# Making the w1 and w2 products of a finished tile inside the Mamba pass of the next one

## The chip, the cores and the metric

One core of a Trainium2 chip runs the whole program. The metric is device time in microseconds (us): before the change the median of three runs was 3416.43 us (3415.66 to 3416.49). TensorE is called PE here, VectorE DVE, ScalarE ACT, GpSimd POOL and SyncE SP.

## The reference

A Mamba block, then a feed-forward network (FFN) with ternary weights; each adds its input and is followed by a layer norm without weights. Input x is (4, 2048, 256) in float32.

```python
xz = x @ in_proj_w.T; xc, z = xz[..., :512], xz[..., 512:]
u = silu(causal_conv4(xc) + conv_b)
dt_lo, B, C = split(u @ x_proj_w.T)                 # 64, 16, 16
delta = softplus(dt_lo @ dt_proj_w.T + dt_proj_b)
h_t = exp(delta_t * A) * h_{t-1} + delta_t * u_t * B_t
y = (sum_n h * C + u * D) * silu(z)
x1 = layernorm(x + y @ out_proj_w.T)
g = silu((x1 @ w1.T) * s1) * ((x1 @ w2.T) * s2)     # 256 -> 1024
g = gelu((g @ h1.T) * sh1); g = gelu((g @ h2.T) * sh2)   # 1024 -> 1024
out = layernorm(x1 + (g @ w3.T) * s3)               # 1024 -> 256
```

## The kernel before

The work is cut into 16 tiles of 512 positions (4 sequences of 4 tiles). Three parts follow each other, with a barrier between.

**Mamba stage** (`mamba_stage`). A tile holds 64 groups of 128 lanes (32 channels x 4 states). For each group ACT makes the decays exp(delta*A) in one of three PSUM banks (`decay_of`, L560), and DVE runs the scan over 512 positions (L753). For every four groups DVE (L738) or POOL (L640) makes delta*u*B, POOL multiplies the states by C (L630), PE sums over the states (`fold_step`, L409). The order on each engine is written out as 64 slots per pass, numbered i = 0 to 63; a pass also makes the front of the next tile: the convolution (slots 0 to 15), silu of u on ACT (17) and of z (40), the products for z (26 to 33), for x of the tile after the next (47 to 53), the step sizes (24, 38, 54, 6) with their softplus in pieces over seven slots, and the output projection (55 to 60) with the residual sums (58, 59, 61, 62). The layer norm of a tile stands at slots 1 to 11 of the next pass. Each engine works through its slots in order and waits on counting semaphores. SP's queue carries the copies that spread delta and delta*u over partitions through DRAM (`copies`, L245 to L262), the load of x (L284) and the store of x1 (L295). ACT issues no DMA.

**Rounding of the weights** (`round_weights`). All five FFN weights are loaded in 28 pieces, rounded to fp32r on ACT, compared with the unrounded ones on DVE, and the differences are summed on PE. A flag says whether all survived exactly. If so, the split stage below runs, else a float32 stage. With these inputs it is the split stage.

**FFN stage** (`ffn_stage` with `split`). An activation is kept as two fp32r parts, the rounded one ("high", made by a copy on ACT, L1053) and the rest ("low", a subtraction on DVE, L1117), and each product runs over both parts. For each tile PE transposes x1 (L967), makes 8 chunks of w1 and w2 products (64 matmuls, L955), layer 0 (128 matmuls), layer 1 (128) and the output product (L1014). ACT applies silu (L1060) and gelu (L1076), DVE the gate (L1127), the residual and the norm. Two PSUM banks alternate in each layer: product m waits until gelu m-2 has emptied its bank. The w1 and w2 products of the next tile come after the output product of this one.

## Time and profile before

| | |
|---|---|
| median of 3 runs | 3416.43 us |
| the profiled execution, its time / its span | 3414.18 us / 3412.4 us |
| Mamba stage | 0 to about 2034 us |
| rounding of the weights | about 2034 to 2072 us |
| FFN stage | about 2072 to 3412 us |
| busy over the span | PE 78%, DVE 69%, ACT 53%, POOL 50% |
| granted TensorE clock, mean | 0.86 |

The profile is one execution. Busy time leaves out register, branch and DMA-issuing instructions. Row 2 of the profile's page shows two regimes: in slices 1 to 23 DVE and POOL are at 8 to 9 tenths, PE at 5 to 7 and the granted clock at 7 to 8 tenths; from slice 26 on PE is at 9 and the clock at 9 to 10. In timeline rows the bracket at the end gives the idle time before an instruction and who ended it. A float32 matmul is recorded twice.

### The profile page before, as it was taken

To read this page: it belongs to the slowest core of one execution; us is meant where nothing else is said; L and a number is where in the kernel's file an instruction comes from. 1 tells how busy PE (TensorE), PEld (TensorE's weight loads), DVE (VectorE), ACT (ScalarE), POOL (GpSimd) and SP (SyncE) were. 2 spreads that over 40 slices of the span, in tenths; PEclk is the share of its full clock that TensorE was granted. 3 is DMA by queue.
4 is the path that set the end of the run, shared out by engine and by line. 5 is a ranking of instruction groups with operands and counts; after the bars stand their busy time and mean duration, and the time that the engine had idled before them with its cause. 6 is when DMAs were issued, how large, how long until landed. Compare 5 with 4: busy or idle time off the path is not lost. (4 is left out here: it accounts for less than half of the span.)

```text
span 3412.4 us, 36441 instructions
## 1 busy us (share of the span) xinstructions
PE 2663.4 (78%) x10431; PEld 1545.8 (45%) x10432; DVE 2371.1 (69%) x2860; ACT 1819.3 (53%) x2980; POOL 1702.9 (50%) x636
## 2 busy tenths in 40 slices
PE   5766776676676667657667438999999999999997
PEld 2222222122122122212212115888888888888886
DVE  2999999899999899999999964333334334344443
ACT  3657666666666666666666534444444444444442
POOL 0888888898898888888888850000000000000000
PEclk8777877788787787778878657999999999999999
DMA  3344433444433444334444322000000000000000
GB/s 89 80 99 111 111 94 88 104 105 99 107 93 91 105 111 100 91 94 105 99 111 98 88 85 97 13 13 12 13 12 13 12 13 12 13 12 13 12 13 13
DMA packets 138266, 225.74 MB, mean 66 GB/s; under 512 B 14432, under 2 KB 49120, under 8 KB 138080
## 3 DMA queue, kind: packets, MB, share of 16 engines
q1 hardware_dynamic: 138080, 223.80, 26.4%
q14 instruction: 135, 1.11, 0.1%
q8 instruction: 51, 0.84, 0.1%
HBM read 173.42 MB, written 50.33 MB: 66 GB/s over the span
## 5 line engine op out<-in xcount | busy, mean ns | idle before, releaser
L753 DVE TENSOR_TENSOR_SCAN h<-bank,state,db 128x512 f32<-128x512 f32 x1024 | 1255.9, 1273 | 84.6 <-POOL hc L630 61.0
L630 POOL TENSOR_TENSOR hc<-h,c_rows 128x2048 f32<-128x2048 f32 x256 | 1159.2, 4533 | 85.1 <-DVE h L753 48.8
L560 ACT ACTIVATE bank<-d_bc,a_neg 128x512 f32<-128x512 f32 x1024 | 699.1, 687 | 595.0 <-DVE h L753 594.0
L955 PE MATMUL s_bank<-s_act,weights_r 128*128 128x512 f32 x4096 | 935.0, 389 | 0.0
L955 PEld LDWEIGHTS s_bank<-s_act,weights_r 128*128 128x128 f32 x4096 | 767.8, 188 | 158.6
L1117 DVE TENSOR_TENSOR s_act<-s_h,s_act 128x512 fp32r<-128x512 f32 x384 | 262.8, 689 | 638.0 <-ACT s_act L1053 625.1
L388 PE MATMUL bank<-bc,w_spread 64*128 64x512 f32 x272 | 157.3, 602 | 449.4 <-DVE db L738 445.7
L1076 ACT ACTIVATE s_h<-s_bank,s_sc 128x512 f32<-128x512 f32 x256 | 176.0, 687 | 528.8 <-PE s_bank L955 528.6
L738 DVE TENSOR_TENSOR db<-bank,du_bc 128x2048 f32<-128x2048 f32 x192 | 436.5, 2273 | 19.8 <-DMA du_bc<-du_rows 19.8
L409 PE MATMUL bank<-hc,fold_w 128*32 128x512 f32 x2048 | 358.9, 782 | 93.5 <-DVE uz L777 78.0
L388 PEld LDWEIGHTS bank<-bc,w_spread 64*128 64x128 f32 x272 | 59.4, 232 | 658.1 <-DVE db L738 571.3
L640 POOL TENSOR_TENSOR db<-du_bc,b_row 128x2048 f32<-128x2048 f32 x64 | 289.5, 4524 | 127.2 <-DVE h L753 90.8
L347 PE MATMUL bank<-xb,w_conv 128*128 128x512 f32 x512 | 291.3, 699 | 6.3 <-DVE res L784 4.6
L1053 ACT ACTIVATE s_act<-s_h 128x512 fp32r<-128x512 f32 x384 | 241.7, 629 | 18.1 <-DVE s_h L1127 9.9
L955 PE MATMUL s_bank<-s_x_t,weights_r 128*128 128x512 f32 x1024 | 236.8, 391 | 1.4 <-DVE s_x_t L1111 1.4
L955 PEld LDWEIGHTS s_bank<-s_x_t,weights_r 128*128 128x128 f32 x1024 | 192.3, 189 | 41.2 <-DVE s_x_t L1111 1.8
L1060 ACT ACTIVATE s_silu<-s_bank,s_sc 128x512 f32<-128x512 f32 x128 | 88.3, 690 | 178.8 <-PE s_bank L955 170.9
L409 PEld LDWEIGHTS bank<-hc,fold_w 128*32 128x32 f32 x2048 | 44.7, 120 | 304.1 <-issue 188.4
L347 PEld LDWEIGHTS bank<-xb,w_conv 128*128 128x128 f32 x512 | 99.7, 215 | 172.8 <-issue 164.8
L322 PE MATMUL bank<-xT_sb,w_in 128*128 128x512 f32 x256 | 147.8, 719 | 19.8 <-DVE a_neg L724 15.7
L361 PE MATMUL bank<-uz,w_xp 128*96 128x512 f32 x128 | 87.4, 797 | 91.9 <-ACT uz L491 91.9
L1127 DVE SCALAR_TENSOR_TENSOR s_h<-s_bank,s_sc,s_silu 128x512 f32<-128x512 f32 x128 | 96.1, 751 | 81.8 <-PE s_bank L955 81.8
(91 smaller groups left out, 2304.1 us busy)
## 6 DMA issues: line engine op xcount, KB each, us to landing
d_bc<-d_rows SPq DMA_DIRECT2D x256, 256.0 KB, 4.4
du_bc<-du_rows SPq DMA_DIRECT2D x256, 256.0 KB, 7.5
d_rows<-sp_r SPq DMA_DIRECT2D x64, 256.0 KB, 2.0
du_rows<-sp_w SPq DMA_DIRECT2D x64, 256.0 KB, 2.0
xT_sb<-in_xT SPq DMA_DIRECT2D x16, 512.0 KB, 9.0
x_nat<-in_x SPq DMA_DIRECT2D x16, 512.0 KB, 4.6
x<-res SPq DMA_DIRECT2D x16, 512.0 KB, 3.2
s_x_nat<-x SPq DMA_DIRECT2D x16, 512.0 KB, 4.4
```

What stands on the lines that cost most here:

```text
L347: last = pe.matmul(p_mm[j % 2][:], w_conv[:, j, k, :], xb[:, j, k:k + NT], start=k == 0, stop=k == TAPS - 1)
L388: pe.matmul(dst[:], spread_w[:, which, :], bc[t.tt % 2][DTR:P, :], start=True, stop=True).then_inc(done, 1)
L409: last = pe.matmul(p_y[GD * j:GD * j + GD, :], fold_w[:], hc[:, k % HCSTEPS, j, :], start=q == 0, stop=q == QN - 1, tile_position=(0, GD * j))
L560: act.activation(decays[DECAY_BANK[g]][:], d_bc[c % 2][:, j, :], ACT.Exp, scale=a_neg[:, g:g + 1]).then_inc(decay, 1)
L630: pool.tensor_tensor(hc[:, k % HCSTEPS], h[:, H_SLOT[k]], c_rows[:, q, :].unsqueeze(1).broadcast_to([P, JC, NT]), ALU.mult).then_inc(hc_do ...
L640: pool.tensor_tensor(db[:, k % DBSTEPS], du_bc[c % 2][:], b_row[:].unsqueeze(1).broadcast_to([P, JC, NT]), ALU.mult).then_inc(db_pool, 1)
L738: dve.tensor_tensor(db[:, k % DBSTEPS], p_b[:].unsqueeze(1).broadcast_to([P, JC, NT]), du_bc[c % 2][:], ALU.mult).then_inc(db_dve, 1)
L753: dve.tensor_tensor_scan(h[:, H_SLOT[k], j, :], decays[DECAY_BANK[g]][:], db[:, k % DBSTEPS, j, :], state[:, g:g + 1], ALU.mult, ALU.add). ...
L955: last = pe.matmul(dst, weights[:, w_at + k * rows_w + cols:w_at + k * rows_w + cols + P], ins[j][:, k, :], start=k == 0 and j == 0, stop= ...
L1053: act.activation(acts[(c // KH) % 2][0][:, c % KH, :], hring[c % 3][:], ACT.Copy).then_inc(hi, 1)
L1076: act.activation(dst, p_h[m % 2][:], ACT.Gelu, scale=sc[:, 2 + layer, m:m + 1]).then_inc(gelu, 1)
L1117: dve.tensor_tensor(a[1][:, c % KH, :], hring[c % 3][:], a[0][:, c % KH, :].bitcast(F32), ALU.subtract).then_inc(lo, 1)
```

## The change

- After the norm of a tile, in the next pass, PE transposes its rows into two PSUM banks (slots 13 to 20, by fp32 matmuls with the identity), ACT takes the high part with the sign turned, PE adds it back on a second transposition, ACT takes the low part. Then 16 products of 4 matmuls (8 chunks of w1, 8 of w2) stand at the slots in `AB_PLACES`; ACT empties each bank one slot later and issues its store to DRAM (`ab`) two slots later, and loads the next weight chunk from DRAM (`w12`) after every second one. The first pass does this for a tile of zeros; after the last pass a list of slots with nothing else in it does it for the last tile.
- w1 and w2 are rounded once at the start by ACT and put into `w12`.
- x is loaded into the residual's own buffer `res`, after the store of x1 and the transposes; DVE's two waits before the residual are dropped.
- The FFN stage (`split_stage`) loads `ab`; silu of the next tile's chunk m on ACT, the gate and its low part on DVE stand in layer 0 of this tile behind gelu m. PE has only layer 0, layer 1 and the output product. DVE's norm comes right after the residual. The rounded w1 and w2 are no longer kept, only checked. The float32 stage stays as it was.

```diff
+XT_PLACES = ((13, 2), (17, 1))
+AB_PLACES = ((25, 0), (30, 2), (32, 2), (34, 2), (35, 1), (36, 2), (38, 1), (40, 1), (41, 0), (44, 2), (46, 2),
+             (48, 2), (50, 2), (52, 2), (60, 2), (62, 2))
...
@@ SP, Mamba stage
-                sp.wait_ge(out_sb, t.count(SUB, OUT0))
-                sp.sem_inc(waited, 1)
-                sp.dma_start(x_nat[:], x[t.b, rows, :].rearrange("(s p) c -> p s c", p=P)).then_inc(x_in, 16)
                 copies(t, 3)
+                sp.wait_ge(x1_out, t.count(16, 16))
+                sp.wait_ge(xt_mm, t.count(KM, KM))
+                sp.dma_start(res[:], x[t.b, rows, :].rearrange("(s p) c -> p s c", p=P)).then_inc(x_in, 16)
@@ PE, Mamba stage
+            def ffn_product(t, e):
+                nxt = t.following()
+                m, which = divmod(e, 2)
+                if e == 0:
+                    pe.wait_ge(xt_lo, xt_done(t, KM))
+                if which == 0:
+                    pe.wait_ge(w12_in[m % 2], t.count(16 * KH // 2, 16 * (m // 2 + 1)))
+                before = product_before(t, e)
+                if before is not None:
+                    pe.wait_ge(ab_sb, ab_done(t, before + 1))
+                if exists(nxt):
...
+                    elif e in (1, 9, 14):
+                        pe.wait_ge(sp_dve, nxt.count(2 * KI, 2 + 2 * (1, 9, 14).index(e)))
+                for k in range(KM):
+                    for j in range(2):
+                        last = pe.matmul(product_bank(t, e)[:], w12_sb[m % 2][:, which, k, :], x_t[j][:, k, :],
+                                         start=k == 0 and j == 0, stop=k == KM - 1 and j == 1)
+                last.then_inc(ab_mm, 1)
@@ ACT, Mamba stage
+            def store(t, e):
...
+                act.wait_ge(ab_sb, ab_done(t, e + 1))
+                act.dma_start(at, ab_sbuf[e % 2][:]).then_inc(ab_out[e % 2], 16)
...
+                for e in range(AB):
+                    if i == AB_PLACES[e][0] + 1:
+                        act.wait_ge(ab_mm, t.count(AB, e + 1))
+                        act.wait_ge(ab_out[e % 2], t.count(16 * AB // 2, 16 * (e // 2) + ABOUT0))
+                        act.activation(ab_sbuf[e % 2][:], product_bank(t, e)[:], ACT.Copy,
+                                       scale=-1.0).then_inc(ab_sb, 1)
+                        m = e // 2 + 2
+                        if e % 2 == 1 and m < KH:
+                            load_w12(t, m)
...
@@ DVE, Mamba stage
-                dve.tensor_tensor(res[:, s, :], p_mm[s % 2][:, 0:DM], x_nat[:, s, :], ALU.add).then_inc(out_sb, 1)
+                dve.tensor_tensor(res[:, s, :], p_mm[s % 2][:, 0:DM], res[:, s, :], ALU.add).then_inc(out_sb, 1)
...
-                        if i == SUM_SLOTS[0]:
-                            dve.wait_ge(ln_out, t.count(SUB, SUB))
-                            dve.wait_ge(x1_out, t.count(16, 16))
@@ SP, FFN stage (split_stage)
             def tile(t):
+                nxt = t.following()
+                if exists(nxt):
+                    sp.wait_ge(summed, t.count(SUB, SUMMED0))
+                    load(nxt)
+                    for m in range(KH):
+                        sp.wait_ge(gate_lo, nxt.count(KH, m - RING + 1))
+                        load_products(nxt, m)
+                sp.wait_ge(ln_out, t.count(SUB, SUB))
...
@@ ACT, FFN stage (split_stage)
+            def gated(t, m):
+                act.wait_ge(ab_in[m % RING], t.count(16 * KH // RING, 16 * (m // RING + 1)))
+                a = abr[m % RING][:, 0, :]
+                act.activation(a, a, ACT.Silu, scale=sc[:, 0, m:m + 1]).then_inc(silu, 1)
+                if m:
+                    gate_high(t, m - 1)
+                if m == KH - 1:
+                    gate_high(t, m)
...
+            def hidden(t, layer):
+                dst = (mid, ends[t.tt])[layer][0]
+                for m in range(KH):
+                    c = layer * KH + m
+                    act.wait_ge(h_mm, t.count(L2, c + 1))
+                    act.wait_ge(lo, t.count(L2, c - RING + 1 + LO0))
+                    act.activation(hring[c % RING][:], p_h[m % 2][:], ACT.Gelu,
+                                   scale=sc[:, 2 + layer, m:m + 1]).then_inc(gelu, 1)
+                    act.wait_ge(gelu, t.count(L2, c + 1 + GELU0))
+                    act.activation(dst[:, m, :], hring[c % RING][:], ACT.Copy).then_inc(hi, 1)
+                    if layer == 0 and exists(t.following()):
+                        if m == 0:
+                            act.wait_ge(o_mm, t.count(SUB, OUT0))
+                        gated(t.following(), m)
```

How the instructions stand now. First ACT in the FFN stage, layer 0, chunk after chunk. `s_h` is the gelu's output, `s_act` and `s_mid` the high part, `s_abr` a loaded pair of products, `s_end` the gate's high part. Before:

```order
L1072 REGISTER_ALU [waits s_h_mm]
L1076 ACTIVATE s_h<-s_bank,s_sc 128x512 [waits s_lo]
L1052 REGISTER_ALU
L1053 ACTIVATE s_act<-s_h 128x512 [waits s_gelu]
L1072 REGISTER_ALU [waits s_h_mm]
L1076 ACTIVATE s_h<-s_bank,s_sc 128x512 [waits s_lo]
```

and in the changed kernel:

```order
L1218 ACT_TABLE_LOAD [waits s_lo]
L1218 ACTIVATE s_h<-s_bank,s_sc 128x512 [waits s_h_mm]
L1220 REGISTER_ALU
L1221 ACTIVATE s_mid<-s_h 128x512 [waits s_gelu]
L1205 ACT_TABLE_LOAD
L1205 ACTIVATE s_abr<-s_abr,s_sc 128x512 [waits s_ab_in2]
L1199 REGISTER_ALU
L1200 ACTIVATE s_end<-s_abr 128x512 [waits s_gate]
```

Each chunk now holds a silu, a second copy and two table loads; before, silus and gelus stood in two blocks with one load each.

Second, SP at the edge of a tile in the FFN stage, in the loop. Before:

```order
L921 ISA [waits s_summed]
L921 DMA s_x_nat<-x 128x4x256
L932 ISA [waits s_ln_out]
L932 DMA out<-s_res 128x4x256
```

and in the changed kernel:

```order
L1106 ISA [waits s_summed]
L1106 DMA s_x_nat<-x 128x4x256
L1122 ISA
L1111 ISA [waits s_gate_lo]
L1111 DMA s_abr<-ab 128x2x512
...
L1111 ISA [waits s_gate_lo]
L1111 DMA s_abr<-ab 128x2x512
L1127 ISA [waits s_ln_out]
L1127 DMA out<-s_res 128x4x256
```

The eight loads of the next tile's products stand between its x_nat and the store of this tile, and in the next round behind that store.

Third, ACT in the Mamba stage at slots 35 to 37. Before, only decays (L560) stand there:

```order
L559 REGISTER_ALU
L560 ACTIVATE bank<-d_bc,a_neg 128x512 [waits scanned]
L559 REGISTER_ALU
L560 ACTIVATE bank<-d_bc,a_neg 128x512 [waits scanned]
L567 ACTIVATE state<-h 128x4 [waits scanned]
```

and in the changed kernel (L678 is the decay, L738 the eviction, `w_1<-w` the weight load, `ab<-ab` the store):

```order
L678 ACTIVATE bank<-d_bc,a_neg 128x512 [waits scanned]
L735 REGISTER_ALU
L738 ACTIVATE ab<-bank 128x512 [waits ab_out1,ab_mm]
L716 DMA w_1<-w 128x512
L721 REGISTER_ALU
L722 ISA [waits ab_sb]
L722 DMA ab<-ab 128x512
L677 REGISTER_ALU
L678 ACTIVATE bank<-d_bc,a_neg 128x512 [waits scanned]
```

Between two decays ACT now has an eviction, up to two DMA issues and a wait for its own eviction.

## Rows read from the trace of the kernel before

**Rows 1.** Windows: stretch, length, busy of each engine, clock, DMA share, GB/s.
```profile
core 0: us, PE busy (x) PEld busy (x) DVE busy (x) ACT busy (x) POOL busy (x), PEclk, DMA share, GB/s
1269.80:1307.90 38.10, 22.77 (x70) 7.17 (x71) 34.09 (x29) 27.17 (x46) 32.81 (x10) 0.64 0.47 110
...
2100.00:3300.00 1200.00, 1191.91 (x5726) 1004.34 (x5725) 470.59 (x1054) 503.13 (x760) 0.00 (x0) 1.00 0.04 13
```

**Rows 2.** Chain of waits, start of the FFN stage and one tile.
```profile
2082.60 59.84 PE s_bank L955 x256
...
2166.35 58.06 PE s_bank L955 x256
...
2225.28 14.54 PE s_bank L955 x64
2239.92 0.70 ACT s_h L1076
...
2242.05 6.25 PE s_bank L1014 x50
2248.31 58.06 PE s_bank L955 x256
```

**Rows 3.** Timeline of SP's queue, Mamba stage: start, length.
```profile
1143.12 1.76 SPq L253 DMA_DIRECT2D d_bc<-d_rows  x4
...
1229.36 0.41 SPq L295 DMA_DIRECT2D x<-res  x1
...
1350.31 0.41 SPq L295 DMA_DIRECT2D x<-res  x1
```

**Rows 4.** Timeline of DVE in one Mamba tile, instructions after a wait.
```profile
1229.82 3.64 DVE L753 TENSOR_TENSOR_SCAN h<-bank,state,db 128x512 f32<-128x512 f32 x3 [1.40 <-ACT bank L560]
...
1241.56 0.75 DVE L777 SCALAR_TENSOR_TENSOR uz<-uz,dpar,bank 128x512 f32<-128x512 f32 x1 [2.37 <-PE bank L409]
...
1278.94 1.28 DVE L753 TENSOR_TENSOR_SCAN h<-bank,state,db 128x512 f32<-128x512 f32 x1 [3.80 <-POOL hc L630]
```

**Rows 5.** Timeline of ACT, FFN stage.
```profile
2240.64 0.63 ACT L1053 ACTIVATE s_act<-s_h 128x512 fp32r<-128x512 f32 x1
2241.29 1.28 ACT L1060 ACT_TABLE_LOAD   x1
...
2251.09 0.69 ACT L1060 ACTIVATE s_silu<-s_bank,s_sc 128x512 f32<-128x512 f32 x1 [1.13 <-PE s_bank L955]
2251.68 0.62 ACT L1053 ACTIVATE s_act<-s_h 128x512 fp32r<-128x512 f32 x1
```

**Rows 6.** Chain of waits after the last output product.
```profile
3394.66 0.44 DVE s_res L1146
...
3402.34 0.65 DVE s_res L1172 x2
```

**Rows 7.** Timeline of SP's queue at a tile edge, FFN stage.
```profile
2190.71 0.40 SPq L932 DMA_DIRECT2D out<-s_res  x1
2191.48 0.39 SPq L921 DMA_DIRECT2D s_x_nat<-x  x1
```

**Rows 8.** DMA issues: size, median us from issue to landing.
```profile
d_rows<-sp_r SPq DMA_DIRECT2D x64, 256.0 KB, 2.0
...
s_x_nat<-x SPq DMA_DIRECT2D x16, 512.0 KB, 4.4
...
stage<-in_w2T SPq DMA_DIRECT2D x2, 512.0 KB, 5.9
```

**Rows 9.** Groups by form, ACT: busy, mean ns, idle before.
```profile
L560 ACT ACTIVATE bank<-d_bc,a_neg 128x512 f32<-128x512 f32 x1024 | 699.1, 687 | 595.0 <-DVE h L753 594.0
...
L479 ACT ACTIVATE uz<-bank 128x512 f32<-128x512 f32 x64 | 37.4, 584 | 21.0 <-PE bank L334 21.0
```

**Rows 10.** Timeline of PE, Mamba stage: the same eight records twice.
```profile
1116.23 1.94 PE L409 MATMUL bank<-hc,fold_w 128*32 128x512 f32 x8
...
1122.31 1.06 PE L409 MATMUL bank<-hc,fold_w 128*32 128x512 f32 x8
```

**Rows 11.** Timeline of SP's queue, the last store of x1.
```profile
2031.36 0.40 SPq L295 DMA_DIRECT2D x<-res  x1
```

More of the change, by code:

```diff
@@ L430, in project, with transpose, transposed @@
                     last.then_inc(out_mm, 1)
+            def transpose(dst, k, alone):
+                for s in range(SUB):
+                    last = pe.matmul(dst[:, s * P:(s + 1) * P], res[:, s, k * P:(k + 1) * P], w_id[:].bitcast(F32),
+                                     start=s == 0, stop=alone and s == SUB - 1)
+                return last
+            def transposed(t, k, step):
+                dst = bank[XT_PLACES[k][1]]
+                if step == 0:
+                    if k == 0:
+                        pe.wait_ge(ln_out, t.count(SUB, SUB))
+                        pe.wait_ge(sp_dve, t.count(2 * KI, 2 * KI) if exists(t) else t.count(2 * KI, 0))
+                    elif exists(t.following()):
+                        pe.wait_ge(conv_sb, t.following().count(KI, KI))
+                    transpose(dst, k, True).then_inc(tr_mm, 1)
+                elif step == 2:
+                    pe.wait_ge(xt_hi, t.count(KM, k + 1))
+                    transpose(dst, k, False)
+                    pe.matmul(dst[:], w_id[:], x_t[0][:, k, :], start=False, stop=True).then_inc(xt_mm, 1)
@@ new lines, in split_stage @@
+    p_h, p_o = bank[0:2], bank[2:4]
+    consts_in, stored = sem("consts_in"), sem("stored")
+    x_in = [sem("x_in0"), sem("x_in1")]
+    ab_in = [sem(f"ab_in{i}") for i in range(RING)]
+    h_mm, o_mm = sem("h_mm"), sem("o_mm")
+    silu, gate, gate_hi, gate_lo = sem("silu"), sem("gate"), sem("gate_hi"), sem("gate_lo")
+    gelu, hi, lo = sem("gelu"), sem("hi"), sem("lo")
+    scaled, summed = sem("scaled"), sem("summed")
+    ln_dve, ln_out = sem("ln_dve"), sem("ln_out")
+    waited = sem("waited")
@@ new lines, in _, with body, gate_high, hidden @@
+    @block.scalar
+    def _(act):
+        def body():
+            act.wait_ge(consts_in, 16 * 5)
+            act.sem_inc(gelu, GELU0)
+            def gate_high(t, m):
+                act.wait_ge(gate, t.count(KH, m + 1))
+                act.activation(ends[t.tt][0][:, m, :], abr[m % RING][:, 1, :], ACT.Copy).then_inc(gate_hi, 1)
+            def gated(t, m):
[6 more added lines that the diff above has]
+                    gate_high(t, m)
+            def hidden(t, layer):
+                dst = (mid, ends[t.tt])[layer][0]
+                for m in range(KH):
+                    c = layer * KH + m
[9 more added lines that the diff above has]
+                        gated(t.following(), m)
+            for m in range(KH):
+                gated(first, m)
+            with act.Fori(0, STEPS - 1) as b:
+                for tt in range(2):
+                    hidden(PairTile(b, tt), 0)
+                    hidden(PairTile(b, tt), 1)
+            for t in last_pair:
+                hidden(t, 0)
+                hidden(t, 1)
+        branch(act, body)
@@ L971, in gated @@
             def gated(t):
-                pe.wait_ge(xt_lo if split else xt_hi, t.count(KM, KM))
+                pe.wait_ge(xt_sb, t.count(KM, KM))
                 for m in range(KH):
@@ L981, in hidden @@
                 w_at = (H1_AT, H2_AT)[layer]
-                done = lo if split else (gate, gelu)[layer]
                 def arrived(k):
-                    if split:
-                        pe.wait_ge(lo, t.count(L3, layer * KH + k + 1))
-                    elif layer == 0:
+                    if layer == 0:
                         pe.wait_ge(gate, t.count(KH, k + 1 + 2))
@@ L1008, in output @@
                         if s == 0:
[L1009 to L1016 removed]
+                            pe.wait_ge(gelu, t.count(2 * KH, KH + k + 1 + 2))
+                        last = pe.matmul(p_o[s % 2][:, 0:DM], acts[0][:, k, s * P:(s + 1) * P],
+                                         weights[:, W3_AT + k * DM:W3_AT + (k + 1) * DM],
+                                         start=k == 0, stop=k == KH - 1)
                     last.then_inc(o_mm, 1)
@@ L1123, in gated @@
                     dve.wait_ge(silu, t.count(KH, m + 1 + 2))
[L1124 to L1127 removed]
+                    dve.scalar_tensor_tensor(out=acts[0][:, m, :], in0=p_w2[m % 2][:], scalar=sc[:, 1, m:m + 1],
                                              in1=silu_t[m % 2][:], op0=ALU.mult, op1=ALU.mult).then_inc(gate, 1)
[L1129 to L1139 removed]
             def residual(t):
@@ L1229, in _ @@
                     act.wait_ge(loaded[i % ring], 16 * (i // ring + 1))
-                    act.activation(weights[:, at[i]:at[i] + cols[i]], stage[i % ring][:, 0:cols[i]],
-                                   ACT.Copy).then_inc(rounded, 1)
+                    if 2 <= i and at[i] < ROUNDED_FROM:
+                        act.wait_ge(took, i - 1)
+                    act.activation(place(i), stage[i % ring][:, 0:cols[i]], ACT.Copy).then_inc(rounded, 1)
             @block.vector
```

398 lines of the change are left out of this document (311 added, 87 removed).

## Prediction

> **What bounds the kernel now.** I read the stage windows first. From 2100 to 3300 us (the FFN stage) PE is busy 1191.91 of 1200 us at a granted clock of 1.00 (2.4 GHz), ACT 503 and DVE 471 [rows 1]. The chain of waits then shows the repeating tile: 256 matmuls in 58.06 us, 64 more in 14.54 us, about 2.2 us through ACT and DVE after the last (2239.82 to 2242.05), then the rest of the output product; from one 256-piece to the next is 81.97 us [rows 2]. A split matmul costs 58.06/256 = 0.227 us. 15 such periods and a shorter last tile are the stage, so every matmul taken out pays, as long as PE stays the bound.
>
> The Mamba stage is different. A tile takes 120.95 us (one store of x1 to the next [rows 3]). DVE runs the scans and waits only three times per tile: 1.40 us for ACT, 2.37 us for PE, 3.80 us for POOL [rows 4]. ACT has room on average, but makes the decays in line with everything else. So here added work costs nothing until ACT or PE, which work in order, make DVE late.
>
> **FFN stage: PE's work goes, ACT's grows.** Removed per tile: 64 matmuls, 14.5 us, and the transposes, 0.9 us (the gap between the 58.06 piece's end at 2224.41 and 2225.28), 15.4 us. If PE stayed the bound, a tile would take 81.97 - 15.4 = 66.6 us.
> But ACT now works silu of the next tile between the gelus of layer 0, and the order shows an ACT_TABLE_LOAD before each silu and before each gelu: 16 per tile against 2. One costs 1.28 us [rows 5]. From starts in the trace: gelu to copy 0.72, copy to load 0.65, load 1.30 (with its gap), silu to copy 0.59, copy 0.65, load 1.30: 5.21 us per chunk [rows 2, 5]. PE needs 16 x 0.227 = 3.63 us for it. With two banks PE can't run ahead, so layer 0 goes at ACT's pace.
>
> The Trainium skill ("ScalarE: Activation LUTs", section "What ACT_TABLE_LOAD costs") puts a drain of about 1.38 us on top of the 1.28 us of a load. The trace shows none: the copy that starts at 2240.64 runs 0.63 us and the load starts at 2241.29 [rows 5]. With that drain a tile would be 15 switches x 1.38 = 21 us longer; the sum goes by the rows. The same page's advice to do all of one table set before switching is the order that this change gives up.
>
> The tile edge, counted from the end of the output product (T0). The loads for the next tile's silus stand on SP behind x_nat's, and that behind the store of out, which waits for the norm. The norm ends 8.3 us after T0 (3394.66 to 3402.99) [rows 6]. SP starts the store 0.2 us later, x_nat 0.77 us after that start, 0.39 us long [rows 7]; with 0.3 us for the instructions between, the first ab load (512 KB) is issued at 10.0. It lands 2.0 us later at best (a 256 KB store alone), 4.4 (x_nat's 512 KB) or 5.9 us (512 KB behind others) [rows 8]. I take 4.9, since store and x_nat are in flight: L = 14.9 (12.0 to 15.9). ACT has done gelu 0 by 4.3 and stands before silu 0 until L; gelus 1 to 7 are behind it.
> - gelu 1 starts at L + 0.72 + 1.30 = L + 2.0, gelu 7 six chunks later, L + 33.3.
> - After it copy, load, silu 7, a copy, a copy that waits for DVE's gate, load: gelu 8 starts 6.1 us later and ends at L + 40.1.
> - PE waits for gelu 8 before product 10; products 10 to 15 are 6 x 3.63 = 21.8, the output 8.5 (2239.82 to 2248.31): T0 of the next tile is L + 70.3 = 85.2 us (82.3 to 86.2). That is 3.2 us more than before, not 15.4 less.
>
> Tile 0 finds its loads done and has only the chunk pace: gelu 1 at 8.9 instead of 16.9, so 77.1 us (-4.9). Tile 15 has no next: 66.5 as before. Start of the stage: before, hidden layer 0 started 14.5 us after 2082.60, at 2097.1 [rows 2]; now the first products arrive at about 2079, the last pair must wait for a ring place (a load each 4.4 us after a low part) and lands near 2092.5, so the first product ends near 2095.5, as if started at 2091.9: -5.2. Stage: -5.2 - 4.9 + 14 x 3.2 = **+35 us** (-6 to +49).
>
> **Mamba stage: added per pass.** 64 split matmuls (14.5 us at full clock, up to twice that at half), 16 fp32 transposes of 128x128 and 2 products with the identity (about 5 us); on ACT 4 + 16 evictions of 0.584 us, 16 stores and 8 loads issued from its own queue. SP's issues take 1.76/4 = 0.44 us each [rows 3]; I take that for ACT.
> The dense stretch is slots 35 to 55. In a tile of before (1269.80 to 1307.90) ACT was busy 27.17 of 38.10 us, idle 10.9 [rows 1]. Added there: 11 evictions 6.4, 17 DMA issues 7.5, 11 waits for its own eviction before the store about 0.15 each 1.6: 15.5. That is 4.6 us too many. ACT's lead (a decay may be made when the scan three before ends: 2 x 1.28 - 0.69 = 1.9 us [rows 4, 9]) absorbs 1.9 of it: 2.7 us. PE in the same stretch gets e9 to e13 (4.5 us) among the x products and is held behind DVE by its new wait for sp_dve; it wins back some from a clock that doesn't fall (eight folds took 1.94 us after an idle gap, 1.06 later [rows 10]). I put 1.5 us on the residual. At slots 14 to 20 the evictions of the transposes stand ahead of silu_u (two, 1.2 us), which PE's fold and DVE's 2.37 us stall wait for: 1.2 us. Sum 5.4 us per pass; bounds: -1 (clock gained, all else hidden) and 12 (PE's stall and ACT's overflow in full, evictions also waiting 2.0 us for stores to land two or three times). 15 full passes 81, the last, without a following tile, 3: **+84 us** (-15 to +180). POOL's 3.80 us stall may swallow a part that comes before it; where it does, ACT's table loads of silu_z come late instead.
> x into res: its wait for x1_out and the transposes ends near slot 20, and the next thing queued behind it on SP is the copy of slot 31, and DVE needs x at slot 58: nothing. The waits dropped on DVE were long met: nothing.
>
> **Once.** Start: rounding w1 and w2 falls in ACT's gaps between convolution evictions, +2 us (0 to 8). Tail: after the last norm (stored at 2031.36 [rows 11]) nothing covers the last tile's products. Transposes in two rounds with their evictions, 8 us; 16 products where each pair must evict, issue and land a store (0.6 + 0.44 + 2.0) or a weight load: about 1.5 us each, 24; less what the x1 store took anyway, +2 landing: **+33 us** (25 to 45). Rounding of the weights is the same 28 pieces.
>
> Sum, against the profiled execution's own span 3412.4: 35 + 84 + 2 + 33 = +154, span 3566; its time was 1.8 us above its span (3414.2), so 3568. The median of the runs is 2.2 above that execution: **3570 us**, 4.5% slower.
>
> **The rivals.**
> A: *the Mamba pass hides its additions.* For: the places lie where PE has gaps, ACT is idle 28% of the dense stretch, and PE's clock is only 0.64 there [rows 1], so it can gain. Against: ACT's overflow by count. Then 1 us per pass: 16 instead of 84, 3502.
> B: *faster.* The point is L: below 11.7 us a tile is under 81.97. If the first loads were there when ACT wants silu 0 (6.3 us), every tile were at 77.1: -5.2 - 15 x 4.9 = -79, and with 16 + 2 + 33 from A it is 3416 - 28 = 3388. For: 512 KB landed in 4.4 us. Against: SP's order puts the load behind a norm of 8.3 us.
> C: *the change does what it says.* PE stays the bound at 66.6: -5 - 15 x 15.4 = -236, with 84 + 35: 3299. Only if the table loads cost nothing, against [rows 5].
> D: *worse.* ACT's issues cost twice SP's or it waits for landed stores (12 us per pass, 180), and PE, idle 6 us at each tile edge, falls to half clock, which doubles the product after layer 0 (+3.6 x 14 = 50): 3570 + 96 + 50 = 3716; either half alone 3620 to 3666.
> E: the drain of the skill's page on each switch: by the page's figure 15 tiles x 21 = 310 us more, 3880. By the rows there is no gap to put it in.
>
> **Chances.** Forecast 0.57, A 0.17, B 0.06, C 0.02, D 0.15, E 0.01, and 0.02 for an even end between A and B. Within 0.2% of 3416 (7 us, about what a measurement of this kernel tells from no change) 0.02; slower 0.90; faster 0.08. Range for 8 in 10: A's 3502 less its stage's lower bound gives 3490; up to a half of D, 3650. All rest on cases of one sign but B and C.
>
> **What would show it.** Tile period in the FFN stage near 85 with a PE gap of some 6 us after the third product of layer 0, ended by ACT, and ACT's silu 0 ended by the DMA of ab; ACT_TABLE_LOADs at 5.2 us pace; PE busy about 78% of the stage. If ab's load is not the wait, the period is 77 (B). In the Mamba stage: the store of x1 every 126 us instead of 120.95, DVE's idle before the scan put down to ACT above 1.4 us per tile; a period of 122 is A, over 130 is D. Between the last x1 store and the first weight load 33 us more. The forecast is wrong if layer 0 runs at 3.63 us per chunk, or if the Mamba period falls.

## Result and the profile after

| | before | after |
|---|---|---|
| time, median of 5 runs | 3416.30 us | 3752.34 us |
| lowest, highest | 3415.66, 3416.49 | 3735.57, 3758.72 |
| profiled execution, time and span | 3414.2, 3412.4 | 3735.57, 3733.7 |
| granted clock, mean | 0.86 | 0.875 |

The ratio is 1.0977, interval [1.0954, 1.1001]: 9.8% slower. The forecast was 3570 (3490 to 3650), so the sign was right and the size was less than half of it. The profiled execution is the fastest of the five; the sums below are made in its trace.

The stages of the trace of after. The first row is 14 periods of the Mamba stage, the second the FFN stage with some 35 us of the rounding before it, then two stretches of one tile behind the wait at its edge.
```profile
core 0: us, PE busy (x) PEld busy (x) DVE busy (x) ACT busy (x) POOL busy (x), PEclk, DMA share, GB/s
279.03:2178.37 1899.34, 1439.47 (x4927) 612.88 (x4927) 1590.63 (x1414) 1227.73 (x2122) 1493.83 (x547) 0.85 0.50 136
2300.00:3600.00 1300.00, 1047.54 (x4639) 828.91 (x4640) 493.48 (x1068) 791.32 (x977) 0.00 (x0) 0.93 0.21 72
3059.80:3069.70 9.90, 9.84 (x32) 7.59 (x32) 4.09 (x6) 9.73 (x12) 0.00 (x0) 0.75 0.19 59
3070.30:3090.00 19.70, 15.28 (x62) 11.31 (x62) 8.19 (x12) 19.38 (x23) 0.00 (x0) 1.00 0.25 80
```
PE was busy 99% of the FFN stage [rows 1]; now 81% (1047.54 of 1300). In the Mamba stage the granted clock was 0.85 over the 14 periods, against 0.78 over the same 14 before (258.51 to 1955.73), so it rose with the added work.

SP's queue of after: the stores of x1 (L341, the first, fifteenth and last of 16), then the first load of the FFN stage's weights (L1625).
```profile
279.03 0.42 SPq L341 DMA_DIRECT2D x<-res  x1
...
2178.37 0.40 SPq L341 DMA_DIRECT2D x<-res  x1
2255.84 0.40 SPq L341 DMA_DIRECT2D x<-res  x1
...
2295.62 0.82 SPq L1625 DMA_DIRECT2D stage<-in_w1T  x2
```
From the first to the fifteenth are 14 periods of 135.67 us, against 121.23 before (258.51 to 1955.73). The last is 77.5 against 75.6. So the 321.3 us between the spans lie here:

| part | measured | forecast |
|---|---|---|
| up to the first x1 store (one pass and the rounding of w1, w2) | +20.5 | +7 |
| 14 periods x 14.44 | +202.1 | +76 |
| last interval | +1.8 | +3 |
| x1's last store to the first weight load: 39.8 against 3.4 | +36.4 | +33 |
| rounding and FFN stage (to the end of the span) | +60.4 | +35 |

The Mamba tile from 1229.96 to 1365.22: DVE's longest waits, each in the brackets of the instruction behind it (one of 1.06 us for ACT at 1250.11 is not shown).
```profile
1230.42 3.64 DVE L939 TENSOR_TENSOR_SCAN h<-bank,state,db 128x512 f32<-128x512 f32 x3 [1.55 <-ACT bank L678]
1243.31 0.75 DVE L963 SCALAR_TENSOR_TENSOR uz<-uz,dpar,bank 128x512 f32<-128x512 f32 x1 [3.52 <-PE bank L464]
...
1278.67 1.28 DVE L939 TENSOR_TENSOR_SCAN h<-bank,state,db 128x512 f32<-128x512 f32 x1 [1.66 <-ACT bank L678]
1283.41 1.28 DVE L939 TENSOR_TENSOR_SCAN h<-bank,state,db 128x512 f32<-128x512 f32 x1 [3.46 <-ACT bank L678]
1289.21 1.28 DVE L939 TENSOR_TENSOR_SCAN h<-bank,state,db 128x512 f32<-128x512 f32 x1 [1.14 <-ACT bank L678]
1296.14 0.70 DVE L946 SCALAR_TENSOR_TENSOR bank<-sp_w,bank 128x512 f32<-128x512 f32 x1 [5.65 <-ACT bank L651]
...
1321.41 1.28 DVE L939 TENSOR_TENSOR_SCAN h<-bank,state,db 128x512 f32<-128x512 f32 x1 [2.92 <-ACT bank L678]
```
Before, DVE waited three times [rows 4]. POOL's 3.80 is gone, which the forecast had named as possible; the first two grew by 1.3 in all (forecast 1.2). New are five waits for ACT between 1278 and 1322, 14.8 us: 14.8 + 1.3 - 3.8 are 12.3 of the 14.3 by which this tile is longer. The longest of them, 5.65, stands behind silu_z with its two table loads (1289.19 to 1293.7 on ACT); before, the same work ran while DVE waited 3.80 for POOL. What ACT did there:
```profile
1276.72 0.60 ACT L738 ACTIVATE ab<-bank 128x512 f32<-128x512 f32 x1 [2.43 <-DMA ab<-ab]
1277.48 0.34 ACTq L722 DMA_DIRECT2D ab<-ab  x1
...
1281.21 0.60 ACT L738 ACTIVATE ab<-bank 128x512 f32<-128x512 f32 x1 [2.45 <-DMA ab<-ab]
...
1282.42 1.30 ACT L678 ACTIVATE bank<-d_bc,a_neg 128x512 f32<-128x512 f32 x2 [0.62 <-ACT ab L738]
```
The eviction of a product (L738) waits 2.4 us for its place, the SBUF buffer whose last store (L722) has not landed; the decays (L678) stand behind it. PE in the same stretch:
```profile
1281.86 2.07 PE L428 MATMUL bank<-xd,w_dt 64*128 64x512 f32 x2 [7.22 <-ACT ab L738]
...
1296.68 0.79 PE L443 MATMUL bank<-bc,w_spread 64*128 64x512 f32 x1 [6.01 <-ACT ab L738]
1297.40 1.93 PE L464 MATMUL bank<-hc,fold_w 128*32 128x512 f32 x8
```
PE waits for the same evictions to free a bank (`pe.wait_ge(ab_sb, ...)` in `step_sizes` and `rows`), its fold (L464) behind that, POOL behind the fold, and ACT's silu_z starts late (1289.19) with softplus behind it.

The FFN stage, ACT at a tile edge, and PE behind it. T0 is 3041.5.
```profile
3046.55 1.28 ACT L1205 ACT_TABLE_LOAD   x1
3057.07 0.72 ACT L1205 ACTIVATE s_abr<-s_abr,s_sc 128x512 f32<-128x512 f32 x1 [9.24 <-DMA s_abr<-ab]
...
3059.82 0.63 ACT L1221 ACTIVATE s_mid<-s_h 128x512 fp32r<-128x512 f32 x1
3060.47 1.28 ACT L1205 ACT_TABLE_LOAD   x1
```
```profile
3059.84 9.84 PE L1162 MATMUL s_bank<-s_end,weights_r 128*128 128x512 f32 x32 [7.46 <-ACT s_h L1218]
3070.28 3.92 PE L1162 MATMUL s_bank<-s_end,weights_r 128*128 128x512 f32 x16 [0.59 <-ACT s_h L1218]
3075.50 3.96 PE L1162 MATMUL s_bank<-s_end,weights_r 128*128 128x512 f32 x16 [1.30 <-ACT s_h L1218]
```
Silu 0 waits for the load of ab until T0 + 15.6 (forecast 14.9), PE has a gap of 7.5 us (forecast some 6), and then a chunk takes 5.22 us (3070.28 to 3075.50; forecast 5.21). The stores of out are 86.78 us apart on average (13 periods); forecast 85.2. The gelus of this tile start 5.22 us apart from 3059.10 on, also while the matmuls behind the gap take longer. PE's next wait is at the edge between the layers, for DVE's low part of the last chunk (gelu 7 at 3090.43, copy, subtraction). The granted clock is 0.50 again from 3092.5 to 3095.0:
```profile
3092.56 27.48 PE L1162 MATMUL s_bank<-s_mid,weights_r 128*128 128x512 f32 x114 [3.14 <-DVE s_mid L1268]
```

### The profile page after: what moved, and what is told of

The parts are those of the page before. It is cut to its first block and busy times, and to the rows that moved or that the text cites. A ratio compares the mean times of both kernels' runs of the same rounds, so it can differ in the third digit from the quotient of the medians.

```text
span 3733.7 us, 39363 instructions
## 1 busy us (share of the span) xinstructions
PE 2866.8 (77%) x10945; PEld 1656.0 (44%) x10946; DVE 2362.1 (63%) x2829; ACT 2269.8 (61%) x3508; POOL 1708.9 (46%) x636
## 5 line engine op out<-in xcount | busy, mean ns | idle before, releaser
L678 ACT ACTIVATE bank<-d_bc,a_neg 128x512 f32<-128x512 f32 x1024 | 694.6, 686 | 412.0 <-DVE h L939 313.6
L1162 PE MATMUL s_bank<-s_end,weights_r 128*128 128x512 f32 x2048 | 518.6, 411 | 172.8 <-ACT s_h L1218 156.0
L1162 PE MATMUL s_bank<-s_mid,weights_r 128*128 128x512 f32 x2048 | 491.6, 401 | 68.1 <-DVE s_mid L1268 47.0
L1162 PEld LDWEIGHTS s_bank<-s_end,weights_r 128*128 128x128 f32 x2048 | 398.7, 198 | 288.0 <-ACT s_h L1218 182.6
L1162 PEld LDWEIGHTS s_bank<-s_mid,weights_r 128*128 128x128 f32 x2048 | 393.6, 194 | 165.9 <-DVE s_mid L1268 53.4
L530 PE MATMUL bank<-x_t,w 128*128 128x512 f32 x1088 | 384.8, 486 | 35.4 <-ACT ab L738 25.0
L464 PE MATMUL bank<-hc,fold_w 128*32 128x512 f32 x2048 | 340.2, 743 | 19.3 <-DVE uz L963 17.6
L530 PEld LDWEIGHTS bank<-x_t,w 128*128 128x128 f32 x1088 | 222.1, 220 | 232.6 <-issue 125.2
L738 ACT ACTIVATE ab<-bank 128x512 f32<-128x512 f32 x272 | 160.7, 591 | 233.8 <-DMA ab<-ab 128.8
L1268 DVE TENSOR_TENSOR s_end<-s_h,s_end 128x512 fp32r<-128x512 f32 x128 | 88.6, 692 | 332.8 <-ACT s_end L1221 332.8
L1256 DVE SCALAR_TENSOR_TENSOR s_abr<-s_abr,s_sc 128x512 f32<-128x512 f32 x128 | 96.2, 752 | 258.1 <-ACT s_abr L1205 258.1
L1268 DVE TENSOR_TENSOR s_mid<-s_h,s_mid 128x512 fp32r<-128x512 f32 x128 | 88.5, 692 | 214.0 <-ACT s_mid L1221 214.0
```

The lines of the kernel that those rows point to most:

```text
L464: last = pe.matmul(p_y[GD * j:GD * j + GD, :], fold_w[:], hc[:, k % HCSTEPS, j, :], start=q == 0, stop=q == QN - 1, tile_position=(0, GD * j))
L530: last = pe.matmul(product_bank(t, e)[:], w12_sb[m % 2][:, which, k, :], x_t[j][:, k, :], start=k == 0 and j == 0, stop=k == KM - 1 and j ...
L678: act.activation(decays[DECAY_BANK[g]][:], d_bc[c % 2][:, j, :], ACT.Exp, scale=a_neg[:, g:g + 1]).then_inc(decay, 1)
L1162: last = pe.matmul(p_h[m % 2][:], weights[:, at:at + P], ins[j][:, k, :], start=k == 0 and j == 0, stop=k == KH - 1 and j == parts - 1)
```

## Experiments

The same Mamba code in three kernels (e2, e4, e11) had periods of 129.55, 130.32 and 130.91 us, so a difference below 1.4 us is not read, and one of 1.65 is only just above that. Mamba periods are means of 14, from the stores of x1; FFN periods are means of 13 or 14, from the stores of out. Each run has one execution but e11 and e12. The FFN stage of e5 and e7 to e9 works on other data of the same size, and e3, e5 and e7 to e10 leave out or shorten work, so only times and waits are read from them.

| run | Mamba | FFN tile | time |
|---|---|---|---|
| before | 121.23 | 81.97 | 3416.3 |
| after | 135.67 | 86.78 | 3752.3 |
| e1 four places; early loads | 130.53 | 77.79 | 3530.3 |
| e2 four places, later stores; grouped silus | 129.55 | 70.01 | 3396.7 |
| e3 half of the products; gelu for silu | 135.28 | 75.03 | 3551.2 |
| e4 all edits of e1 and e2 | 130.32 | 70.01 | 3408.0 |
| e5 short evictions and stores | 135.22 | 87.01 | 3731.4 |
| e6 other pairs, other places | 130.47 | 68.15 | 3382.1 |
| e7 no stores, no weight loads | 126.21 | 87.05 | 3587.8 |
| e8 transposes alone | 122.88 | 87.24 | 3515.7 |
| e9 no stores | 128.81 | 87.27 | 3627.5 |
| e10 no weight loads | 135.95 | 87.03 | 3738.1 |
| e11 best candidate | 130.91 | 68.16 | 3386.6 (4 runs) |
| e12 the same, x in two halves | 128.66 | 68.17 | 3357.5 (4 runs) |

**First four.**

> Two edits of the changed kernel, one for each stage. Mamba: four places to evict products into instead of two (the two others are the halves of res, which are free until x is loaded; x's load goes behind the second chunk's copies on SP). Theory (ACT stands before an eviction until the store two before it has landed, and PE, which works in order, stands behind ACT): the waits of the eviction for a landed store, 97.7 us over 13 tiles or 7.5 us per pass, and part of PE's wait for a free bank go; the pass falls from 135.7 to 125 to 129 us. Rival (what costs is the number of evictions and DMA issues on ACT, or PE's added work): the waits go but the pass stays at 132 us or more. FFN: SP issues the first four loads of products of the tile after next before it waits for the norm and the store. Theory (the period is chunk pace plus the load that stands behind the norm): silu 0 no longer waits 9.24 us, and the period falls from 86.7 to 77 to 78 us. Rival (the pace of 5.2 us is itself set by loads): the gap comes back at later silus and the period stays over 83. Whole time about 3490 by the theories.

```diff
-        ab_sbuf = [sb(f"ab{i}", [P, NT]) for i in range(2)]
+        ab_sbuf = [sb(f"ab{i}", [P, NT])[:] for i in range(2)] + [res[:, 2 * i:2 * i + 2, :]... for i in range(2)]
+AB_BUF = (0, 1, 2, 3, 0, 1, 2, 3, 0, 1, 0, 1, 0, 1, 0, 1)
...
@@ SP, FFN stage, ahead of its wait for ln_out
+                if exists(nxt.following()):
+                    for m in range(RING):
...
+                        load_products(nxt.following(), m)
```
The waits for landed stores shrink, and the period falls 5.1 us, to 130.53 where 125 to 129 were expected. FFN: 77.79, the tile edge worth 9.0 us of the 9.24 that silu 0 waited.

> Mamba: four places as in the run before, and each store is issued one slot later, so that ACT doesn't stand before it for its own eviction (0.62 us of idle before the next decay, 16 times per pass). Theory: 2 to 6 us per pass less than with four places alone, 121 to 126 us. Rival (the issue itself costs ACT that time): no more than 1 us less. FFN: silus of the next tile in four pairs behind gelus 4, 7, 10 and 13 of the sixteen, loads as in the changed kernel. Theory (table loads set the pace of layer 0, and the wait at the tile edge is only felt because silu 0 stands before gelu 1): 8 table loads instead of 16, spread where PE has two products in hand, first silu 15 us after the tile edge: PE is the bound again, period 66 to 68 us. Rival (the table loads stall PE wherever they stand): 5.1 us of ACT for each pair against two banks, period over 72. Whole time about 3310 by the theories.

```diff
-                    if i == AB_PLACES[e][0] + 2:
+                    if i == min(AB_PLACES[e][0] + 3, NG):
...
+    SILU_AFTER = (3, 6, 9, 12)
...
-                    if layer == 0 and exists(t.following()):
+                    if c in SILU_AFTER and exists(t.following()):
+                        at = 2 * SILU_AFTER.index(c)
...
+                        gated(t.following(), at)
+                        gated(t.following(), at + 1)
```
The later stores give no more than the spread between runs, where 2 to 6 us were expected. ACT's waits of its decays for its own evictions (0.62 us each, 73.9 us over 14 passes in e1) are gone, and the period stays: other waits covered them. The number is the one of my rival, that the issue itself costs ACT the time; e12 speaks against its reason. FFN: 70.01, 16.8 less, though the loads still stand behind the norm; e4 with early loads has 70.01 too. Both are 2 us over what was expected, and the whole times, about 3310 expected, are some 90 us over, from both stages; PE still waits 3.2 us per tile (rows at e6).

> Four places, stores one slot later, silus in four pairs, and the early loads of products. Against the second run it differs only by the early loads. Theory: with the pairs behind the fourth gelu the load was no longer waited for, so nothing changes, 66 to 68 us per tile. Rival (part of the period left is still the tile edge): 2 us or more less than in the second run. Whole time about 3310.

> Changed kernel with two alterations that change its output. Mamba: the products of w1 and w2 leave out the low part of x, 32 matmuls per pass instead of 64; buffers, evictions, stores as they are. Theory (landed stores and in-order waits): PE's busy time falls by 7 to 14 us per pass, but the pass only by 0 to 4 us, 132 to 136. Rival (PE's added work is what makes the pass long): 8 us or more less, 127 or under. FFN: the silus are computed as gelus, so that no table is loaded; the loads of products stay behind the norm. Theory: the pace after the first chunk is PE's 3.63 us, silu 0 still waits until about 15.6 us after the edge, product 3 starts near 17.6: period 17.6 + 13 x 3.63 + 8.5 = 73 us. If the table loads were not the pace: 84 or more. Whole time about 3500 if only the FFN part falls.

```diff
-                    for j in range(2):
+                    for j in range(1):
-                        act.activation(a, a, ACT.Silu, ...
+                        act.activation(a, a, ACT.Gelu, ...
```
Half of the products' matmuls gone from PE, and the period stays (135.28): with the stores in place, PE's added work is not what makes it long. With no table to load, the FFN tile is 75.03 (expected 73); PE waited once at the edge and then ran through:
```profile
3031.28 20.98 PE L1162 MATMUL s_bank<-s_end,weights_r 128*128 128x512 f32 x80 [5.62 <-ACT s_h L1218]
```
80 matmuls in 20.98 us are 0.262 each, against 0.227 before, 2.8 us more in all. The granted clock was 0.50 (the lower of its two levels) from 3031.2 to 3035.3, behind the gap of 5.62 us, and 1.00 from 3040 on. Here PE sets the pace, so the slow matmuls can account for the 2.0 us over what was expected; in layer 0 of after the gelus set it. The whole times of e1 and e3 are 40 and 51 us above what was expected.

**Second four.** What was still open: whether ACT's own work, the bytes stored, the DMAs, or the transposes carry the Mamba part.

> Changed kernel, in which only the first 64 of the 512 columns of each product are evicted and stored (the products, the waits and the number of instructions and stores are as they are; the FFN stage then loads other finite data of the same size in place of the products, so its output is not the reference's and its time should not change: 86 to 87 us per tile). Pass of 135.7 us. Theory (volume: 16 evictions of 0.58 us on ACT and the time that stores need to land): an eviction of 64 columns should take some 0.25 us, 5 us less per pass on ACT, and a store lands in about 2 us instead of 3: the pass falls by 6 or more, to 130 us or less. Rival (coupling: ACT and PE wait for each other's place in order, whatever an eviction takes): 132 to 135.

```diff
-                        act.activation(ab_sbuf[e % 2][:], product_bank(t, e)[:], ACT.Copy, ...
+                        act.activation(ab_sbuf[e % 2][:, 0:64], product_bank(t, e)[:, 0:64], ACT.Copy, ...
-                act.dma_start(at, ab_sbuf[e % 2][:])
+                act.dma_start(at[:, 0:64], ab_sbuf[e % 2][:, 0:64])
```
The groups of evictions on ACT, first of after and then of this run:
```profile
L738 ACT ACTIVATE ab<-bank 128x512 f32<-128x512 f32 x272 | 160.7, 591 | 233.8 <-DMA ab<-ab 128.8 <-PE bank L530 103.8 <-ACT ab L738 0.5
```
```profile
L738 ACT ACTIVATE ab<-bank 128x64 f32<-128x64 f32 x272 | 59.1, 217 | 260.8 <-DMA ab<-ab 137.0 <-PE bank L530 123.4 <-issue 0.4
```
ACT has 102 us less to do (6.0 per tile), and the period falls by 0.45, to 135.22, just above the rival's bound. The waits take it all back: they end when a store lands, and a store of an eighth of the bytes still needs most of the time. Landing in the Mamba stage, of after and of this run:
```profile
ab<-ab ACTq DMA_DIRECT2D x224, 256.0 KB, 3.7
```
```profile
ab<-ab ACTq DMA_DIRECT2D x224, 32.0 KB, 2.6
```
The 3.7 itself varies: with the same stores e3 and e10 have medians of 3.1 and 3.0. My theory of volume is wrong here; the rival holds.

> Changed kernel, in which the 16 stores of products and the 8 loads of w1 and w2 of each pass are left out (the products are made from the first two pieces, evicted, and overwritten; the FFN stage loads other finite data of the same size). Everything that waits for one of these DMAs, and the time to issue them on ACT, is gone; the products and evictions are all there. Pass of 135.7 us. Theory (half to two thirds of the 14.4 us is DMA: landed stores, loads that PE waits for, issues): 125 to 129 us. Rival 1 (nearly all of it is DMA): 121 to 124. Rival 2 (work and order alone): 131 or more.

> Changed kernel without the products, their evictions and their DMAs: of the additions to a pass only the transposes of x with their four evictions, x in res, and the waits remain (the FFN stage loads other finite data). Pass of before 121.2 us, of the changed kernel 135.7. Theory: the transposes cost 1 to 3 us (the forecast had 1.2): 122 to 124 us. Rival (the transposes and the waits for them at slots 13 to 20, with the fold and silu_u behind them, are a large part): 126 or more.

```diff
@@ e7
-                act.dma_start(at, ab_sbuf[e % 2][:]).then_inc(ab_out[e % 2], 16)
-                            load_w12(t, m)
...
@@ e8, also
-                last.then_inc(ab_mm, 1)
+                pe.sem_inc(ab_mm, 1)
```
In both, the loads for the tile after go too, and nothing waits for a landed store or load any more; in e8 the eight matmuls of a pair and the evictions become increments of their semaphores, so PE and ACT still wait for each other in the same order, and the 1.65 us of e8 hold that too. Both land where the theory put them: 122.88 with the transposes and that order, 126.21 with products and evictions.

> As the run with all edits, with two alterations. FFN: the pairs of silus stand behind gelus 2, 5, 10 and 13 instead of 4, 7, 10 and 13, so that none stands before the last chunk of a layer; the early loads stay, since silu 0 is now wanted some 6 us after the tile edge. In the run before, PE waited 1.7 us per tile at the edge between the layers for the low part, 0.9 for a gelu and 0.5 at the output: 3.2 of 70.0. Theory: the 1.7 go, 68 to 68.8 us per tile; rival (the wait at the layer edge is ACT's and DVE's own latency): 69.8 or more. Mamba: the eviction of the fourteenth product waited 3.5 us for a store that took 8.7 us to land behind the broadcasts; five evictions now use other places (AB_BUF), so that no place comes again within four slots there. Theory: that wait and the scan's stall of 2.8 behind it go, pass 126.5 to 128.5 us; rival (it is covered by other waits): 129 to 130.5.

```diff
-    SILU_AFTER = (3, 6, 9, 12)
+    SILU_AFTER = (1, 4, 9, 12)
-AB_BUF = (0, 1, 2, 3, 0, 1, 2, 3, 0, 1, 0, 1, 0, 1, 0, 1)
+AB_BUF = (0, 1, 2, 3, 0, 1, 2, 3, 0, 1, 2, 0, 1, 0, 1, 0)
```
PE's waits over 13 FFN tiles, in e2 and in this run (12 tiles):
```profile
PE s_bank L1172 <- DVE s_mid L1280: 22.4, 13, 1.7
PE s_bank L1172 <- ACT s_h L1228: 12.3, 13, 0.9
PE s_bank L1185 <- DVE s_end L1280: 6.5, 13, 0.5
```
```profile
PE s_bank L1181 <- ACT s_h L1237: 11.4, 12, 1.0
PE s_bank L1194 <- DVE s_end L1289: 6.1, 12, 0.5
```
The wait at the layer edge is gone, 1.86 us per tile. The new places failed: 130.47. ACT in one Mamba tile of this run, the twelfth product's store and the fourteenth product's eviction, which uses the same place:
```profile
1263.65 0.34 ACTq L729 DMA_DIRECT2D ab<-ab  x1
...
1272.07 0.60 ACT L747 ACTIVATE ab<-bank 128x512 f32<-128x512 f32 x1 [3.48 <-DMA ab<-ab]
```
and SP's queue just before:
```profile
1259.76 1.84 SPq L301 DMA_DIRECT2D d_bc<-d_rows  x4
1261.87 1.73 SPq L310 DMA_DIRECT2D du_bc<-du_rows  x4
```
The store was issued behind eight broadcasts of 256 KB, with the load of x (512 KB) issued 0.36 us after it, and took 8.4 us to land; the median of such stores was 3.9 in this run. How far apart two uses of a place must be depends on what another queue moves at that moment. Which of the two, broadcasts or load of x, slowed it was not taken apart.

**Last four.**

> Changed kernel, in which only the 16 stores of products of each pass are left out; the 8 loads of w1 and w2 are issued from ACT as before (the FFN stage loads other finite data of the same size). Without stores and loads the pass took 126.2 us, with both 135.7; four places instead of two gave 5.1 of these 9.5. Theory (nearly all is the eviction that waits for a landed store): without stores 126.5 to 128.5 us. Rival (the loads that PE waits for and that share the queue with the broadcasts cost as much): 130 or more.

> Changed kernel, in which only the loads of w1 and w2 are left out of the passes (every product is made from the first two pieces, so the output is not the reference's); the stores are all there, from two places. Theory (stores are what counts): the pass stays at 134 to 136 us. Rival (loads count as much as stores): 132 or less.

The edits are the two halves of e7's. Without stores 128.81, a little over what was expected; without the loads 135.95, no change. One after the other: before 121.23, transposes +1.65, products and evictions +3.33, weight loads +2.60, stores +6.86. The loads cost 2.6 only where the stores don't stand in front, so these parts hold for this order of adding them.

DVE's waits, added up by what ended them over the 14 periods and divided by 14 (us per pass), follow the periods:

| DVE waits for | before | e8 | e7 | e9 | after | e12 |
|---|---|---|---|---|---|---|
| ACT: decay, before a scan | 1.4 | 1.5 | 1.4 | 1.4 | 11.2 | 1.5 |
| ACT: softplus of the step sizes | 0.2 | 0.2 | 2.2 | 3.7 | 5.7 | 3.1 |
| PE: fold | 2.3 | 3.2 | 4.5 | 4.1 | 4.2 | 4.3 |
| DMA: broadcast of delta*u | 0.3 | 0.0 | 0.1 | 1.6 | 0.6 | 1.8 |
| POOL, before a scan | 3.8 | 3.8 | 3.9 | 3.9 | 0.0 | 3.9 |
| ACT: B and C | 0.0 | 1.0 | 0.7 | 0.7 | 0.4 | 0.7 |
| sum | 8.0 | 9.7 | 12.8 | 15.4 | 22.0 | 15.2 |

Products and evictions (e8 to e7) come to DVE as later softplus and later folds; its scans wait for ACT no longer than before. The weight loads (e7 to e9) come as 1.5 us of broadcasts that land later and 1.5 of softplus. The stores (e9 to after) come as decays that are late.

> Four places (the first assignment), stores one slot later, silus in pairs behind gelus 2, 5, 10 and 13, early loads of products. It should give the sum of what was measured apart: pass 129.5 to 130.5 us, FFN tile 68.15 us, 3370 to 3385 us whole, ratio to the kernel before 0.986 to 0.991.

> As the run before it, but x is loaded into res in two halves, each behind the last store from that half, so that the four places go round through the twelfth product and the fourteenth takes a place that was last stored from four products before. In the runs before, the fourteenth eviction waited 3.5 us for a store issued right behind the broadcasts (8.2 us to landing), and a scan stalled 2.8 us behind it. Theory: that wait goes and 2 to 3 us of the pass with it, 127 to 128.5 us, whole time 3340 to 3360. Rival (another stall takes its place, as with the first new assignment): 129.5 or more, 3370 to 3385.

```diff
+AB_BUF = (0, 1, 2, 3, 0, 1, 2, 3, 0, 1, 2, 3, 0, 1, 0, 1)
-                sp.dma_start(res[:], x[t.b, rows, :]...).then_inc(x_in, 16)
+                for k in (0, 1):
+                    sp.wait_ge(ab_out[2 + k], all_stored(t, 2 + k))
+                    sp.dma_start(res[:, 2 * k:2 * k + 2, :], ...).then_inc(x_in[k], 16)
```
e11: 3386.6 us, ratio 0.9906 [0.9890, 0.9923]; its Mamba period is 0.4 and its time 2 us above what was expected. e12: 3357.5 us, ratio 0.9825 [0.9808, 0.9841], some 1.7% below the kernel before, a small gain, but the interval is clear of 1; its time is within the expectation, its period 0.2 above it. The group of DVE's scans, of after, of e9 and of e12:
```profile
L939 DVE TENSOR_TENSOR_SCAN h<-bank,state,db 128x512 f32<-128x512 f32 x1024 | 1256.5, 1265 | 176.7 <-ACT bank L678 172.0 <-POOL hc L815 4.0
```
```profile
L936 DVE TENSOR_TENSOR_SCAN h<-bank,state,db 128x512 f32<-128x512 f32 x1024 | 1254.5, 1270 | 85.7 <-POOL hc L812 61.7 <-ACT bank L678 23.1
```
```profile
L949 DVE TENSOR_TENSOR_SCAN h<-bank,state,db 128x512 f32<-128x512 f32 x1024 | 1253.8, 1269 | 86.1 <-POOL hc L825 61.7 <-ACT bank L686 23.6
```
With all 16 stores issued from ACT, e12's scans wait as if there were none. The evictions of e12, by place:
```profile
L748 ACT ACTIVATE ab<-bank 128x512 f32<-128x512 f32 x170 | 100.2, 589 | 69.2 <-PE bank L538 67.6 <-DMA ab<-ab 1.4
L748 ACT ACTIVATE res<-bank 128x512 f32<-128x512 f32 x102 | 60.2, 590 | 88.4 <-PE bank L538 88.0
```
128.8 us of waits for landings have become 1.4, though the stores land no sooner (from the first two places median 3.9, slowest of all 11.9 us, against 3.7 and 9.7 in after). So the stores' 6.9 us were the wait for their landing and what stood behind it, not their issue.

## Why the prediction came out as it did

- **FFN, chunk pace and tile edge: right.** Load 1.28, pace 5.22, L = 15.6, period 86.78 for 85.2 forecast; e1 and e3 take the two causes apart. The 1.6 us more are 0.7 in L and about 1 at the edge between the layers. There PE stands 3.14 us before the last two matmuls of product 8, and the granted clock is 0.50 from 3092.5 to 3095.0, behind that wait. So product 9 ends at 3098.3, 1.0 us after gelu 8 (3097.3, L + 40.2 as forecast), and product 10 starts 1.0 late. The clock that fell was rival D's, of which the forecast had no share, but not at the place that D named: behind the gap of 7.5 us it fell too and cost nothing, as gelus 1 to 7 kept their 5.22 us. 14 x 1.6 = 22 of the stage's 25 us too little. The page "ScalarE: Activation LUTs" of the Trainium skill (section "What ACT_TABLE_LOAD costs") has a drain of about 1.38 us per switch; here the copy that starts at 3059.82 ends at 3060.45 and the load starts at 3060.47. No drain, as the forecast took it, and rival E (3880) falls.
- **Tail and start: right.** +36.4 for +33. Before the first x1 store e8 is 4.4 us late (262.88 - 258.51), of which one pass's transposes are 1.7: the rounding of w1 and w2 is about 2.7, forecast 2.
- **x into res, and the transposes: no contradiction.** Together they are e8's +1.65; the forecast had nothing and 1.2.
- **Mamba: the step that failed.** "Sum 5.4 us per pass", with "evictions also waiting 2.0 us for stores to land two or three times" kept as an upper bound. The step that failed is the wait for landed stores, which was left at nothing in the sum: the stores cost 6.9 us per pass (128.81 without them, 135.67 with them), the weight loads 2.6. Without stores and loads the pass is 5.0 us longer (e7), which is near 5.4 by luck, as the 5.4 were made of other things. The largest term was ACT's overflow in front of the scans (2.7, out of 17 issues at 0.44 and evictions), but in e7 the scans wait for ACT 1.4 us per pass as before, and e12 shows no cost of the stores' issues. The waits for its own evictions, put at 0.15 us each, measured 0.62, yet taking them away changed nothing (e2). DVE's scans behind ACT's decays, before and in e7 (us in total, times, longest):
```profile
DVE h L753 <- ACT bank L560: 20.0, 14, 1.5
```
```profile
DVE h L932 <- ACT bank L678: 18.5, 13, 1.5
```
The forecast had 12 as its worst and 14.4 came. Two mistakes. The wait was priced by the best landing of the list, 2.0 [rows 8], when a store in after needs 3.7 in the median and up to 9.7 us. The list of before had transfers of the same size beside others, and far slower:
```profile
d_bc<-d_rows SPq DMA_DIRECT2D x256, 256.0 KB, 4.4
du_bc<-du_rows SPq DMA_DIRECT2D x256, 256.0 KB, 7.5
```
And it was added as ACT's own time, when PE and DVE stand behind it in their order, so that one late eviction holds a step size, a fold and a silu too.
- **The sum.** Mamba 224.4 for 86, FFN and rounding 60.4 for 35, tail 36.4 for 33: 321.3 for 154. "Over 130 is D" was met by the trace, and D's price per pass (12) was the nearest. Of its two causes on ACT the landed stores were it and the issues were not: they took 0.34 us each, not twice SP's 0.44.
- **The rivals.** A (the pass hides it) is out: even e8 and e7 are 1.65 and 5.0 longer. B's point, L below 11.7 for a faster tile, is right in kind: with early loads the tile is 77.79, forecast 77.1. C's 66.6 can nearly be had (68.15) once the table loads are grouped.

Left open: who makes the softplus and the folds late in e7 (3.3 us per pass over e8). e3 lets PE's count of matmuls out only while the stores are there, so whether it is PE's time or PE's and ACT's waits for each other's place in order (the evictions of e12 wait 67.6 + 88.0 us for PE) wasn't taken apart. Nor was it for the weight loads whether their issue on ACT has a share in the 2.6 us.

## What to carry to other kernels

Before an engine that others wait for is given a store to issue, ask how many uses later its place comes again, and compare that with the landing time beside the transfers of the other queues, not with the best one in the list. Follow a wait into every in-order engine that stands behind it; busy time and issue count say little about it. And work that needs another activation table costs little in pairs, placed where PE has two products in hand: 16 loads in single file took 5.2 us per chunk, 8 in pairs left PE waiting 1.5 us per tile.
